# Layer two of a group one group later on TensorE, and its message sums two groups ahead

## What is computed

```python
msg = relu(x[src] + edge_attr)
agg = segment_sum(msg, dst, 50000)
h = x + agg
h = relu(relu(h @ W1 + b1) @ W2 + b2)      # W1 128x256, W2 256x128
out = layernorm(x + h)                     # over the 128 features
```

## Time and profile before

| | |
|---|---|
| median of three executions | 476.75 us (476.61 to 477.19) |
| span of the profiled execution | 508.3 us |
| busy: PE, DVE, ACT, POOL | 92%, 81%, 79%, 63% of the span |
| TensorE clock granted, mean | 0.991 of full |
| DMA | 90.89 MB, 177 GB/s over the span at HBM |

### The profile page before, as it was taken

One profiled execution on the slowest core, in us unless ns is written; L12 is line 12 of the kernel. 1 busy time (PEld: TensorE's weight loads), 2 busy tenths in 40 slices (PEclk: granted clock), 3 DMA queues, 4 the chain that ended last, 5 costly groups with the idle time before them and its releaser, 6 DMA issues.

```text
span 508.3 us, 9923 instructions
## 1 busy us (share of the span) xinstructions
PE 469.2 (92%) x2959; PEld 360.2 (71%) x2959; DVE 409.9 (81%) x1539; ACT 399.9 (79%) x881; POOL 320.8 (63%) x315
## 2 busy tenths in 40 slices
PE   5879999999989999989998989989899989989994
PEld 3647777676776777767786767767677867767773
DVE  6567879788797887977887877878778878878885
ACT  2328988797888898877887877878778878878885
POOL 7566766666756676666766656656566666666713
PEclk9979999999999999999999999999999999999999
DMA  5644656655656566655666656657556666656613
GB/s 134 168 135 155 193 185 201 196 175 184 195 173 190 183 206 203 177 174 177 195 199 181 192 173 184 186 172 204 170 183 186 202 182 182 203 173 188 218 58 117
DMA packets 81930, 90.89 MB, mean 179 GB/s; under 512 B 13841, under 2 KB 52372, under 8 KB 81876
## 3 DMA queue, kind: packets, MB, share of 16 engines
q1 hardware_dynamic: 71874, 70.80, 43.3%
q0 software_dynamic: 9728, 19.46, 16.6%
q10 hardware_dynamic: 274, 0.00, 0.0%
HBM read 64.61 MB, written 25.60 MB: 177 GB/s over the span
## 4 chain that ended last, share of the span: by engine, by line
PE 87%; issue 5%; ACT 3%; DVE 2%; another core or an unknown queue 2%; DMA 1%; POOL 0%; SPq 0%; DVEq 0%
PE h_ps L867 33%; PE h1T_ps L859 32%; PE hT_ps L834 13%; PE hT_ps L812 8%; ACT h1T L730 1%; ACT y L749 1%; ACT hT L724 1%; DMA dst_next<-in_dst_dram 1%; ACT msg_hi L718 0%; DVE stats L608 0%; DVE z L601 0%; DVE h L589 0%; DVE before_in_row L288 0%; DVE row_holds L358 0%
## 5 line engine op out<-in xcount | busy, mean ns | idle before, releaser
L109 POOL DMA_INDIRECT x_src<-in_x_dram,src_of x287 | 306.5, 1068 | 165.7 <-ACT hT L724 91.6
L867 PE MATMUL h_ps<-w_sb,h1T 128*128 128x128 f32 x1564 | 195.3, 278 | 3.2 <-ACT h1T L730 3.1
L867 PEld LDWEIGHTS h_ps<-w_sb,h1T 128*128 128x128 f32 x1564 | 183.7, 193 | 5.0 <-ACT h1T L730 4.9
L859 PE MATMUL h1T_ps<-hT,w_sb 128*128 128x512 f32 x392 | 185.7, 596 | 1.6 <-ACT hT L724 1.1
L730 ACT ACTIVATE h1T<-h1T_ps,b_sb 128x512 f32<-128x512 f32 x196 | 128.8, 680 | 55.6 <-PE h1T_ps L859 30.8
L749 ACT ACTIVATE y<-z,shift,rstd 128x128 f32<-128x128 f32 x382 | 165.6, 481 | 1.4 <-DVE shift L628 1.3
L589 DVE TENSOR_TENSOR h<-h_ps,b_sb 128x512 f32<-128x512 f32 x98 | 67.4, 688 | 81.9 <-remote 37.6
L859 PEld LDWEIGHTS h1T_ps<-hT,w_sb 128*128 128x128 f32 x392 | 67.5, 192 | 49.3 <-issue 47.7
L834 PE MATMUL hT_ps<-sel,msg_hi 128*128 128x168 f32 (+1 forms) x281 | 72.9, 293 | 20.8 <-issue 20.8
L608 DVE BATCH_NORM_STATS2 stats<-z 128x6 f32<-128x128 f32 x391 | 85.3, 281 | 0.0
L812 PEld LDWEIGHTS hT_ps<-ident,x_sb 128*128 128x128 f32 (+1 forms) x375 | 46.9, 141 | 50.0 <-issue 49.6
(11 more groups left out here) (115 smaller groups left out, 121.2 us busy)
## 6 DMA issues: line engine op xcount, KB each, us to landing
x_sb<-in_x_dram SPq DMA_DIRECT2D x97, 256.0 KB
out_dram<-y SPq DMA_DIRECT2D x97, 256.0 KB
pre_msg<-in_edge_attr_dram SPq DMA_DIRECT2D x292, 64.0 KB
x_src<-in_x_dram,src_of POOLq DMA_INDIRECT x287
w_sb<-in_w_dram SPq DMA_DIRECT2D x2, 128.0 KB
x_sb<-in_x_dram SPq DMA_DIRECT2D x1, 168.0 KB
out_dram<-y SPq DMA_DIRECT2D x1, 168.0 KB
dst_rows<-in_dst_dram SPq DMA_DIRECT2D x1, 97.7 KB
```

The lines of the kernel that those rows point to most:

```text
L109: nc.gpsimd.indirect_dma_start(out=c["x_src"][:, g % EB, k, :], out_offset=None, in_=x, in_offset=bass.IndirectOffsetOnAxis(ap=c["src_of"] ...
L859: nc.tensor.matmul(h1T_ps[h][:, 0:n, 0:p], w1_sb[:, h * 128:(h + 1) * 128], hT[:, 0:n, 0:p], start=True, stop=True).then_inc(h1_summed, 1)
L867: last = nc.tensor.matmul(h2_ps[g % 2][0:p, t, :], h1T[:, h, t, 0:p], w2_sb[:, h, :], start=(h == 0 and t == 0), stop=(h == HC - 1), skip_ ...
```

## The change

TensorE's loop from group 7 to group 91 becomes `hidden_sum(g)`, `turn_x(g + 2)`, `sum_messages(g + 2)`, `output_sum(g - 1)`. Group 6 (LAG) turns and sums two groups and does no layer two, and group 92 (UNLAG) does layer two of 91 and 92 and turns nothing. hT and h1T get a second buffer in SBUF; from group 7 on the result of layer one lies for every second group in the two PSUM banks of the preparation, and the sums of every second group in the spare bank. VectorE prepares messages further ahead: from group 6 on `select` and `add_edge_attr` are for group g + 5, and the low part for g + 4; in the loop `select` and `low_part` change their places. ScalarE's loop is written anew to match, SyncE loads edge attributes six groups ahead where it was five, and GpSimd's gather for a group waits for the copy of the group four before it where it was three. The check of the input's order moves from group 30 to group 4, with a new wait of TensorE at group 7 for its end. The diff, without declarations of buffers and the ends of ScalarE's loop:

```diff
-CHECKED = 30
+CHECKED = 4
 FAR = float(1 << 20)
 
 
-EB, XB, ZB, YB, SB = 6, 6, 6, 4, 4
+EB, XB, ZB, YB, SB = 8, 7, 6, 4, 4
 X_FIRST, X_AHEAD = 2, 5
-GATHER_AHEAD = 3
+GATHER_AHEAD = 4
 ACT_TILES = 1
-EA_FIRST, EA_AHEAD = 2, 5
+EA_FIRST, EA_AHEAD = 2, 6
+
+LAG = 6
+UNLAG_BACK = 5
...
     def sum_bank(g):
 
+        if g > LAG + 1 and (g - LAG) % 2 == 0:
+            return c["spare_ps"].rearrange("p (t n) -> p t n", t=T)
         return bank_of[g].rearrange("p (t n) -> p t n", t=T) if g in bank_of else hT_ps
...
-    hT = sb("hT", [128, T, 128])
-    h1T = sb("h1T", [128, HC, T, 128])
+    hT = sb("hT", [128, 2, T, 128])
+    h1T = sb("h1T", [128, 2, HC, T, 128])
...
+    def hidden_bank(g, h):
+
+        return c["prep_ps"][h].rearrange("p (t n) -> p t n", t=T) if g > LAG and (g - LAG) % 2 else h1T_ps[h]
...
-        aggregate(1)
+        aggregate(1, 4)
         add_edge_attr(4)
         for g in range(2, LAST):
+            if g == LAG:
+                low_part(g + 2)
+                select(g + 3)
+                edge_attr_there(g + 3)
+                add_edge_attr(g + 3)
+                select(g + 4)
+                low_part(g + 3)
+                edge_attr_there(g + 4)
+                add_edge_attr(g + 4)
+            lagged = g >= LAG
+            ahead = g + (5 if lagged else 3)
             add_bias(g)
-            if inside(g + 2):
+            if lagged:
+                if inside(ahead):
+                    select(ahead)
+            else:
                 low_part(g + 2)
             add_x(g)
             if inside(g - 2):
...
             if g == LAST - 1:
                 shifts(LAST - 2)
             z_free(g + 1)
-            if inside(g + 3):
-                select(g + 3)
-            aggregate(g)
-            if inside(g + 3):
-                add_edge_attr(g + 3)
+            if not lagged:
+                select(ahead)
+            elif inside(g + 4):
+                low_part(g + 4)
+            aggregate(g, ahead)
+            if inside(ahead):
+                add_edge_attr(ahead)
             if g == CHECKED + 1:
-                checks["set_general"](dve)
+                checks["set_general"](dve).then_inc(general_set, 1)
...
+        copy_hT(LAG + 1)
+        high_part(LAG + 2)
+        for h in range(HC):
+            hidden(LAG, h)
+        high_part(LAG + 3)
+        copy_hT(LAG + 2)
+        for g in range(LAG + 1, UNLAG):
+            for h in range(HC):
+                hidden(g, h)
+            copy_hT(g + 2)
+            deviation(g - 3)
+            normalize_all(g - 4, g + 3)
...
             for h in range(HC):
                 if h == 1 and inside(g - 2):
-                    pe.wait_ge(h2_ready, g - 1)
-                nc.tensor.matmul(h1T_ps[h][:, 0:n, 0:p], w1_sb[:, h * 128:(h + 1) * 128], hT[:, 0:n, 0:p],
+                    pe.wait_ge(h2_ready, g - 2 if LAG < g <= UNLAG else g - 1)
+                nc.tensor.matmul(hidden_bank(g, h)[:, 0:n, 0:p], w1_sb[:, h * 128:(h + 1) * 128], hT[:, g % 2, 0:n, 0:p],
                                  start=True, stop=True).then_inc(h1_summed, 1)
...
         for g in range(3, GROUPS):
+            if g == LAG + 1:
+                pe.wait_ge(general_set, 1)
             hidden_sum(g)
-            if inside(g + 1):
+            if g <= LAG:
+                turn_x(g + 1)
+                sum_messages(g + 1)
+            if LAG <= g < UNLAG:
+                turn_x(g + 2)
+                sum_messages(g + 2)
+            elif UNLAG < g < LAST:
                 turn_x(g + 1)
                 sum_messages(g + 1)
             if g == CHECKED:
                 checks["sum_flags"](pe)
-            for h in range(HC):
-                output_sum(g, h)
+            if LAG < g <= UNLAG:
+                for h in range(HC):
+                    output_sum(g - 1, h)
+            if g == UNLAG:
+                pe.wait_ge(h2_ready, g - 1)
+            if g < LAG or g >= UNLAG:
+                for h in range(HC):
+                    output_sum(g, h)
```

More of the change, by code:

```diff
@@ L311, in set_general @@
         dve.wait_ge(flags_summed, 1)
-        nc.vector.reduce_max(c["general"][:, :], sums_ps, AX_X)
+        return nc.vector.reduce_max(c["general"][:, :], sums_ps, AX_X)
     def find_ends(pe):
@@ L460, in main_path @@
     h2_ready = sem("h2_ready")
+    general_set = sem("general_set")
     z_ready = sem("z_ready")
@@ L609, in statistics, with aggregate @@
             last.then_inc(stats_ready, 1)
-        def aggregate(g):
+        def aggregate(g, ahead=None):
             p = partitions(g, c)
@@ L614, in aggregate @@
             for t in range(tiles(g, c)):
-                if t == 1 and g >= 1 and inside(g + 3):
-                    edge_attr_there(g + 3)
+                if t == 1 and ahead is not None and inside(ahead):
+                    edge_attr_there(ahead)
                 last = nc.vector.bn_aggr(mean_var[0:p, g % SB, t, :], stats[0:p, g % SB, t, :])
@@ L729, in hidden @@
             act.wait_ge(h1_summed, g * HC + h + 1)
-            nc.scalar.activation(h1T[:, h, 0:n, 0:p], h1T_ps[h][:, 0:n, 0:p], ACT.Relu, bias=b1_sb[:, h:h + 1]).then_inc(h1_ready, 1)
+            nc.scalar.activation(h1T[:, g % 2, h, 0:n, 0:p], hidden_bank(g, h)[:, 0:n, 0:p], ACT.Relu, bias=b1_sb[:, h:h + 1]).then_inc(h1_ready, 1)
         def deviation(g):
@@ L775, in main_scalar, with normalize_all @@
         high_part(4)
-        for g in range(3, LAST):
+        def normalize_all(g, between=None):
+            for t in range(T):
+                last = normalize(g, t)
+                if t == 1 and between is not None and inside(between):
+                    high_part(between)
+            last.then_inc(y_ready, 1)
+        for g in range(3, LAG):
             for h in range(HC):
                 hidden(g, h)
-            if inside(g - 2):
-                deviation(g - 2)
-            if inside(g + 1):
-                copy_hT(g + 1)
[L783 to L789, removed]
+            deviation(g - 2)
+            copy_hT(g + 1)
+            if inside(g - 3):
+                normalize_all(g - 3, g + 2)
+            else:
+                high_part(g + 2)
+        copy_hT(LAG + 1)
[10 more added lines that the diff above has]
+            normalize_all(g - 4, g + 3)
+        for g in range(UNLAG, LAST):
+            for h in range(HC):
+                hidden(g, h)
+            if g == UNLAG:
+                deviation(g - 3)
+            deviation(g - 2)
+            if g > UNLAG:
+                copy_hT(g + 1)
+            if g == UNLAG:
+                normalize_all(g - 4)
+            if inside(g + 3):
+                high_part(g + 3)
+            normalize_all(g - 3)
         deviation(LAST - 2)
@@ L866, in output_sum @@
             for t in range(tiles(g, c)):
-                last = nc.tensor.matmul(h2_ps[g % 2][0:p, t, :], h1T[:, h, t, 0:p], w2_sb[:, h, :],
+                last = nc.tensor.matmul(h2_ps[g % 2][0:p, t, :], h1T[:, g % 2, h, t, 0:p], w2_sb[:, h, :],
                                         start=(h == 0 and t == 0), stop=(h == HC - 1), skip_group_check=True)
```

4 lines of the change are left out of this document (2 added, 2 removed).

## The result

The changed kernel takes 612.17 us (median of 4, 610.7 to 612.75), the kernel before beside it 476.68 us: 1.285 times as long, with an interval of 1.283 to 1.287. The forecast was 610.0 us in 598 to 630.

The account below looks back on a forecast made before the run. TensorE's own pace, 4.61 us a round, was taken to bound the kernel. The late low part over 84 rounds (131.0 us) and the entry wait (2.3 us) added 133.3 to 476.75, giving 610.0 us, range 598 to 630.

Parts of the forecast that it names:

- What bounds the kernel: Kernel before: plain runs go at TensorE's own 4.61 us a round; nearly all long-round excess, 28.2 us, belongs to the profiled execution.
- The floor of 472.6 us: Lowest time the plain runs could reach if every wait, including those in rounds 1 to 3, were removed.
- The low part: TensorE's rounds 8 to 91: messages wait for VectorE's late low part, period 6.17 us for 4.61, 131.0 us over 84 rounds.
- The wait in round 6: At the entry, TensorE waits for the low part of group 8, 2.3 us more.
- the second rival: TensorE's clock falls as well because of the waits: 635 us with one round in ten low, 867 with all; chance 0.05.
- from round 93 on all is in time: At the exit, round 92 gives VectorE's queue a round's lead, so low parts are in time again; no cost.
- What was costed at nothing: ScalarE's copy behind late messages, GpSimd's gathers, SyncE's loads, TensorE's new waits at 7 and 92: no cost expected.
- The first, not slower: Rival: second buffers and the extra lag fill the 23 long rounds and the low part is in time: 474.7 us; chance 0.05.
- The span was expected at 640 to 665 us: Sign in the profile after: late starts of add_bias in the profiled execution have no cover left and lengthen its span.
- The upper part of the range: Up to 630 us: lateness of add_bias that 0.7 us of cover swallowed now counts, 8 us per 0.1 us a round.

Follow-up runs that it names:

- before_low_late: Kernel before with one swap in VectorE's loop, select directly behind add_bias and the low part behind shifts, no lag or second buffers: 626.3 us beside 529.2.
- low_second_again: Changed kernel with the low part back directly behind add_bias and select behind shifts, rerun in an undisturbed set: 484.7 us beside 475.8, ratio 1.018.
- lag_one_further: Changed kernel, VectorE's order kept, all preparation ahead of the messages one group further (low part for g + 5): 537.9 us beside 509.5.
- lag_copy_again: Changed kernel with the low part behind add_bias and ScalarE's copy of hT behind four tiles and a high part, rerun undisturbed: 484.4 us, ratio 1.019.
- after_again: The changed kernel itself, unaltered, run once more beside a kernel before of 475.8 us: 611.9 us, ratio 1.284.
- lag_smooth: Changed kernel with the low part behind add_bias, plus VectorE and ScalarE reordered at entry and exit to mend the seams: 483.6 us, ratio 1.016.
- lag_low_second: Changed kernel with the low part back directly behind add_bias and select behind shifts, first set: 546.3 us beside 529.2, ratio 1.028.
- lag_low_fourth: Changed kernel with VectorE's order add_bias, select, add_x, low part: 549.8 us beside 529.2, ratio 1.037.
- lag_copy_late: Changed kernel with the low part behind add_bias and ScalarE's copy of hT behind four tiles and a high part: 546.6 us beside 509.5.
- lag_low_first: Changed kernel with the low part of g + 4 ahead of add_bias(g) and select behind shifts: 502.6 us, ratio 1.055.

## Why the prediction was right, step by step

**What bounds the kernel.** Right. The plain runs of before have no long rounds to speak of: the changed kernel's profiled execution is 1.7 us over its span, so that the plain span of before is near 475.0 us, 33 us under the profiled one. Take from it 428.4 us of regular rounds from group 4 on and 9.8 us after layer one of group 97, and 36.8 are left for the way to group 4. The changed kernel, which does the same up to there but for the moved check and deeper buffers, takes 36.2 us for it in one profile and 34.9 in the other. So at most some 2 us of long rounds remain, and the excess of 28 us in the profiled execution was its own. The floor of 472.6 us that I gave for a kernel without waits was not reached by any version.

**The low part.** Right, and by its own terms: 0.20 us to `add_bias`, 2.79 us to the low part for 2.80, 0.61 to the messages, 0.74 to layer two, 1.82 to layer one. The period is 6.16 us for 6.17. From layer one of group 8 (58.24 us) to that of 92 (575.51) it is 517.3 us for 84 rounds, 6.158 each, 130.0 us over 84 x 4.61; the sum had 131.0. The place alone makes it (before_low_late), giving it back takes 127 us away (low_second_again), and its price starts only where the low part ends too late: with its start at 0.81 us into the round, or at 1.42, the common round is 4.61 us, at 2.03 it is 5.19, at 2.99 6.16. That the messages and layer two of the same round close the ring is shown from the other side by lag_one_further.

**The entry.** The wait in round 6 was right, the clock behind it was costed at nothing. The rows of the changed kernel's entry:

```profile
45.68 1.88 PE L914 MATMUL h1T_ps<-hT,w_sb 128*128 128x512 f32 x4
...
49.28 0.55 PE L867 MATMUL spare_ps<-ident,x_sb 128*128 128x128 f32 x3 [0.53 <-DVE sel L563]
51.16 0.35 PE L889 MATMUL spare_ps<-sel,msg_hi 128*128 128x176 f32 x1 [1.33 <-DVE msg_lo L587]
...
51.91 3.42 PE L914 MATMUL prep_ps<-hT,w_sb 128*128 128x512 f32 x4
...
58.24 1.88 PE L914 MATMUL h1T_ps<-hT,w_sb 128*128 128x512 f32 x4
```

Round 6 lasts 6.23 us where its own matmuls need 4.61 - 1.81 + 0.36 + 0.72 = 3.88: 2.35 us, and the sum had 2.3. TensorE turned x with a stop of 0.53 us and stood 1.33 us before the messages of group 8. Then layer one of group 7 took 3.42 us for four matmuls that take 1.88 at the higher level, with a granted clock of 0.54 from 51.91 to 55.13, and round 7 lasts 6.33 us (51.91 to 58.24): 1.72 us that no step had. This is the second rival, in one round; in the 84 rounds with idle time of 1.28 us each the granted clock is 1.00. Round 6 differs from those by 1.86 us of idle time and by having no layer two.

But the fall does not always follow. In lag_copy_again, whose round 6 has the same two stops (0.53 and 1.33 us) and lasts the same 6.23 us, the clock stays at 1.00 in round 7, and round 7 lasts 4.74 us. Of the eleven profiles of lagged kernels seven have a fall in round 6 or 7 and four have none. And in the second profile of the changed kernel, after_again, it fell within round 6: rounds 6 and 7 last 6.86 and 7.24 us, 1.5 us more in all than here. The Trainium skill (TensorE: Matmul & The Clock Gate, What's actually happening) says that the gate follows how busy the engine has lately been; the seven profiles agree with that, the four show that a round like this does not decide it alone. What else does, no run shows.

**The exit.** The forecast said that from round 93 on all is in time. The low part was; another engine wasn't:

```profile
580.80 1.88 PE L914 MATMUL prep_ps<-hT,w_sb 128*128 128x512 f32 x4
...
582.49 0.55 DVE L587 SCALAR_TENSOR_TENSOR msg_lo<-pre_msg,msg_hi 128x384 fp32r<-128x384 f32 x1
...
582.61 1.65 ACT L777 ACTIVATE y<-z,shift,rstd 128x128 f32<-128x128 f32 x4 [0.98 <-DVE shift L640]
...
582.87 0.33 PE L889 MATMUL spare_ps<-sel,msg_hi 128*128 128x176 f32 x1
...
584.16 1.24 ACT L758 ACTIVATE h1T<-prep_ps,b_sb 128x512 f32<-128x512 f32 x2
...
584.88 2.05 PE L922 MATMUL h_ps<-w_sb,h1T 128*128 128x128 f32 x16 [1.12 <-ACT h1T L758]
```

Round 93 lasts 5.97 us, 1.36 over 4.61. Its low part started at 582.49 and the messages at once, but layer two waited 1.12 us for the hidden part of 93 (L758), which stands on ScalarE behind four tiles (L777) that wait for VectorE's shift. I had looked for what VectorE and TensorE do at the end, and had costed ScalarE's queue only by its total. The terms that were measured add up: 130.0 + 2.35 + 1.72 + 1.36 = 135.4 us, and the kernel is 135.5 us slower. An agreement to 0.1 us is luck: by the rows of after_again the same sum is 1.5 us larger, and it reaches layer one of group 6 1.2 us sooner. That the forecast missed by 2.2 us is the sum of a term 1.0 too large and two missing ones of 3.1; had the clock not fallen, its errors would nearly have cancelled.

**What was costed at nothing.** ScalarE's copy behind the late messages, the gathers and the loads cost nothing in the 84 rounds, as said, and of the two new waits neither cost anything in the changed kernel: the check that group 7 waits for starts at 49.88 us and layer one of 7 at 51.91, and layer two of 91 and 92 runs without a stop. In lag_smooth, where less stands ahead of it, the first one cost 0.46 us. The gathers mattered at the entry too: in the changed kernel VectorE waited 0.86 us for gathered rows at 54.20 us, which held up nobody, and in lag_smooth 1.52 us, which hid what was mended ahead of them.

**The rivals.** The first, not slower, and with it the reading of the long rounds as a want of buffers: the Trainium skill (Perfetto Trace Analysis, Optimization Strategy) has repeated gaps on the engine that should be saturated as a possible sign of too few buffers. Here more buffers were there, and the gaps came; low_second_again has the same buffers and no gaps in its 84 rounds. So it wasn't buffers that the gaps of the changed kernel wanted. The span was expected at 640 to 665 us on the ground that late starts of `add_bias` would now count in full. It was 610.1: `add_bias` was never late, 0.20 us in each of the 84 rounds. The upper part of the range rested on that and wasn't needed.

## What to carry to other kernels

When a pipeline is made deeper, write down for each engine which instruction of which group is the last input of the next engine, and count the distance in rounds again: lag and lead can cancel, as here, where the low part stayed tied to the round that wants it. Then only its place in its engine's queue decides, and 2.2 us of harmless work moved ahead of it cost 1.55 us in every round. Before buffers are added against a gap, trace it to the instruction that ends it, and look at what stands ahead of that one in its engine's queue. A buffer that makes room on an engine which isn't late buys nothing.

## What the runs showed of the hardware

The kernel before took from 475.8 to 529.2 us in different sets. The lagged kernels whose undisturbed round is 4.61 us have such rounds in the disturbed sets too, with longer ones between them. In the long ones TensorE's records run on, but the engines that wait for its results start late. lag_low_second, in the set with the kernel before at 529.2 us:

```profile
207.52 1.98 PE L920 MATMUL h_ps<-w_sb,h1T 128*128 128x128 f32 x16
...
209.34 1.88 PE L912 MATMUL prep_ps<-hT,w_sb 128*128 128x512 f32 x4
...
211.60 0.69 DVE L601 TENSOR_TENSOR h<-h_ps,b_sb 128x512 f32<-128x512 f32 x1 [2.60 <-remote]
...
212.32 1.27 ACT L756 ACTIVATE h1T<-prep_ps,b_sb 128x512 f32<-128x512 f32 x2 [1.86 <-PE prep_ps L912]
```

Layer two ends by the records at 209.50 us, `add_bias` starts at 211.60 (the page files the wait under an unknown releaser, "remote"), and ScalarE's hidden part 2.98 us after the start of layer one, where 1.06 us is the usual time. Since the ends of matmuls in the records are modelled, this doesn't tell whether the matmuls ended late or the news of their end came late. The longest such wait is at the entry: in the same profile ScalarE's copy for group 3 starts at 39.91 us, 7.6 us after the records have its messages end. In the six longest rounds of that profile, 9.2 to 10.1 us, the granted clock fell too, to a mean of 0.73 to 0.84. The long rounds of before look the same as the one shown, with the clock at 1.00. In the kernels whose TensorE idles for 0.3 to 1.3 us in each round it was nearly absent: 81 of 84 rounds of lag_low_fourth and 83 of 84 of before_low_late are regular in that same set. That isn't a rule: lag_copy_late, in the third set, idled 0.36 us a round on average and was late in most, though its idle time may be the lateness itself, as it has none in the fourth set. What TensorE does in that time stays open: lag_low_first, which was to bear on it, fell in an undisturbed set.

The kernel before, which keeps TensorE at its limit, can thus be 11% slower in one set than in another. The changed kernel was timed only beside a kernel before at 476.7 and 475.8 us (612.2 and 611.9 us), so how it would fare in a disturbed set wasn't measured. A disturbed set misleads on prices: in the first one the swap costs the kernel before 97 us (626.3 against 529.2), and beside an undisturbed kernel before it would be some 150 (626.3 against 475.8).
